# Order of SyncE's transfers where the two halves of the batch meet

## The reference

```
xn  = layernorm(x)
# attention-like part
xm  = xn * time_mix + shift_by_one_token(xn) * (1 - time_mix)
k   = exp(min(xm @ Wk.T, 60));  v = xm @ Wv.T;  r = xm @ Wr.T
wkv = decaying sum over earlier tokens of k*v      (per channel)
sk  = the same sum of k, + 1e-16
a   = (sigmoid(r) * wkv / sk) @ Wo.T
# FFN-like part
xf  = layernorm(xn) * ln_gamma + ln_beta
Wq  = Wf rounded to -1, 0, 1 by its mean absolute value beta
g   = max(abs(xf)) over ALL batches and tokens
f   = clip(xf * 128 / g, -128, 128) @ Wq * (g * beta / 128)
out = x + a + f
```

## Time and profile before

| | |
|---|---|
| runs shown | 918.77, 922.57, 922.42 us; median 922.42 |
| profiled execution | 919.68 us, of which the span from first to last instruction is 917.9 |
| PE busy | 880.4 us, 96% of the span |
| DVE, ACT, POOL busy | 761.5 (83%), 509.4 (56%), 188.1 us (20%) |
| mean granted TensorE clock | 0.992 |
| DMA | 107.13 MB, mean 117 GB/s |

### The profile page before, as it was taken

The page is one execution under the profiler, slowest core; times in us unless marked ns, Lnnn a source line. Parts: engine busy times, 40 slices in busy tenths (PEclk is TensorE's granted clock), DMA queues, the critical chain, the costliest instruction groups (busy, mean ns, idle before and its releaser), DMA issues.

```text
span 917.9 us, 12736 instructions
## 1 busy us (share of the span) xinstructions
PE 880.4 (96%) x3984; PEld 714.3 (78%) x3984; DVE 761.5 (83%) x1282; ACT 509.4 (56%) x830; POOL 188.1 (20%) x242
## 2 busy tenths in 40 slices
PE   2989999999999999999989999999999999999998
PEld 2768777787878777787867888888888888888886
DVE  5998988889798988889768887887878978789684
ACT  3674757657574757657445363554545544455441
POOL 5442333143242333140010020100201102011000
PEclk9999999999999999999999999999999999999999
DMA  8222415042422415043425443253332532334211
GB/s 275 105 81 80 150 41 186 15 149 69 149 80 77 152 46 181 14 151 112 154 97 185 138 144 111 80 192 137 110 115 107 194 137 92 104 137 138 92 47 46
DMA packets 59841, 107.13 MB, mean 117 GB/s; under 512 B 7712, under 2 KB 7712, under 8 KB 59808
## 3 DMA queue, kind: packets, MB, share of 16 engines
q1 hardware_dynamic: 59808, 106.73, 34.2%
HBM read 64.76 MB, written 41.96 MB: 116 GB/s over the span
## 4 chain that ended last, share of the span: by engine, by line
PE 63%; DVE 18%; issue 9%; ACT 4%; DMA 4%; POOL 1%; SPq 0%; DVEq 0%; ACTq 0%; POOLq 0%
PE kvr L483 12%; PE kvr L485 12%; PE kvr L484 12%; PE out_banks L519 6%; PE out_banks L521 6%; PE out_banks L498 5%; PE out_banks L501 5%; PE out_banks L500 5%; DVE scans L933 4%; DVE bn_stats L796 3%; PE transposed L441 2%; DMA other<-ffn_input 1%; DVE rwkv_lo L953 1%; DVE k_and_kv L923 1%; DVE k_and_kv L949 1%
## 5 line engine op out<-in xcount | busy, mean ns | idle before, releaser
L483 PE MATMUL kvr<-xm_hi,wk_hi 128*128 128x512 f32 x256 | 104.4, 408 | 7.2 <-DVE xm_lo L876 4.6
L1186 POOL TENSOR_TENSOR evacuated<-normed,mix_over_ffn_row 128x512 f32<-128x512 f32 x28 | 36.3, 1296 | 360.0 <-DVE ffn_lo L876 360.0
L483 PE MATMUL kvr<-xm_hi,wv_hi 128*128 128x512 f32 x256 | 102.9, 402 | 1.6 <-DVE k_and_kv L923 1.1
L483 PE MATMUL kvr<-xm_hi,wr_hi 128*128 128x512 f32 x256 | 103.3, 404 | 0.0
L498 PE MATMUL out_banks<-wo_hi,rwkv_hi 128*128 128x512 f32 x256 | 101.9, 398 | 0.5 <-DVE rwkv_lo L953 0.5
L485 PE MATMUL kvr<-xm_hi,wk_lo 128*128 128x512 f32 x256 | 101.5, 396 | 0.0
L501 PE MATMUL out_banks<-wo_hi,rwkv_lo 128*128 128x512 f32 x256 | 101.3, 396 | 0.0
L500 PE MATMUL out_banks<-wo_lo,rwkv_hi 128*128 128x512 f32 x256 | 101.2, 395 | 0.0
L519 PE MATMUL out_banks<-w_ternary,ffn_hi 128*128 128x512 f32 x256 | 100.0, 390 | 1.3 <-DVE ffn_lo L876 1.3
L484 PE MATMUL kvr<-xm_lo,wk_hi 128*128 128x512 f32 x256 | 100.9, 394 | 0.0
L485 PE MATMUL kvr<-xm_hi,wr_lo 128*128 128x512 f32 x256 | 100.4, 392 | 0.0
(11 more groups left out here) (125 smaller groups left out, 1910.7 us busy)
## 6 DMA issues: line engine op xcount, KB each, us to landing
other<-ffn_input SPq DMA_DIRECT2D x64, 256.0 KB, 5.4
x<-in_x SPq DMA_DIRECT2D x15, 1024.0 KB, 5.7
other<-in_x SPq DMA_DIRECT2D x8, 1024.0 KB, 5.7
ffn_input<-evacuated SPq DMA_DIRECT2D x32, 256.0 KB, 4.6
ffn_input<-parked SPq DMA_DIRECT2D x32, 256.0 KB, 2.1
attn_scratch<-x SPq DMA_DIRECT2D x8, 1024.0 KB, 4.3
parked<-attn_scratch SPq DMA_DIRECT2D x8, 1024.0 KB, 7.1
out<-parked SPq DMA_DIRECT2D x8, 1024.0 KB, 5.2
```

The lines of the kernel that those rows point to most:

```text
L483: nc.tensor.matmul(KVR[:, m, :], hi, XH[t][:, ch, :], start=(ch == 0), stop=False)
```

## The change

SP's program only; no other engine's changes, and no transfer is added, dropped or resized.

- The mix input of batch 4 (`load_mix_input(HALF, 1)` with its wait for the last transposes) moves from behind the load of x ahead of the wait for DVE's additions and the store of `x1`.
- The four loads of own0 for batch 4 move out of `batch_b` to right behind the store of `x1`.
- The load of `parked` (with its wait for the ternary matrix) stands between chunk 0 and chunk 1 of them.
- The load of the next x into `x1` comes last, behind chunk 3.

```diff
@@ last batch_a
                     for ch in range(CH):
                         sp.dma_start(ZA[:, ch, :], ffn_in[0, 0, ch]).then_inc(s_fld[ch], 16)
+                    sp.wait_ge(pe_t, slots_before(b, "A", len(SLOTS)))
+                    load_mix_input(HALF, 1)
                 sp.wait_ge(dve_out, BANKS + bank_use(b, "A", "attn1") + Q)
                 sp.dma_start(scratch_t[b, 1], X[1][:, :, :]).then_inc(s_xst[1], 16)
+                if is_last:
+                    for ch in range(CH):
+                        load_ffn_input(HALF, "own0", ch)
+                        if ch == 0:
+                            load_parked()
                 sp.wait_ge(s_xst[1], 16 * b + 16)
                 sp.dma_start(X[1][:, :, :], x_t[b + 1, 1]).then_inc(s_x[1], 16)
+
+            def load_parked():
+                sp.wait_ge(act_q, CH)
+                sp.dma_start(ZB[:, :, :], scratch_t[0, 0]).then_inc(s_park, 16)
@@ batch_b
-                for ch in range(CH):
-                    load_ffn_input(b, "own0", ch)
+                if b > HALF:
+                    for ch in range(CH):
+                        load_ffn_input(b, "own0", ch)
@@ behind the loop over half A
-            sp.wait_ge(pe_t, slots_before(HALF - 1, "A", len(SLOTS)))
-            load_mix_input(HALF, 1)
-            sp.wait_ge(act_q, CH)
-            sp.dma_start(ZB[:, :, :], scratch_t[0, 0]).then_inc(s_park, 16)
```

## The result

The changed kernel takes 912.93 us (median of 5 runs, 912.01 to 913.87), the kernel before 918.93 (5 runs, 917.11 to 922.57). The medians differ by 6.0 us. The ratio over all runs is 0.9921, 95% interval 0.9901 to 0.9941: faster by 0.8%, which would be 7.3 us of 918.93 (5.4 to 9.1). The profiled execution has a span of 911.1 us, where the one before had 917.9. Lines moved: L596, L599, L862, L876, L971 of before are L605, L608, L871, L885, L980.

What follows compares the result with a forecast made beforehand. TensorE was taken as the bound, full except where the halves meet, with ACT waiting 8.21 us for own0 chunk 0. Removing 6.66 us gave 913.0 from the profiled execution, 915.8 from the median; forecast 915.0, range 911.5 to 919.5.

Steps and rivals of the forecast that it cites:

- The sum: Total over all moved transfers at the meeting of the halves: 6.66 us less, 913.0 against the profiled execution.
- the window: Stretch from group 5 of batch 4 to its first output product: 35.68 us before, forecast 29.0 at clock 1.00.
- Batch 5 as the yardstick: Batch 5's same stretch, 29.02 us without TensorE gaps, gives the gain; shifted by 123.36 us, its engine starts show what is late next.
- The landing of chunk 0: Own0 chunk 0 behind the store of `x1`: lands 5.5 us after issue, about 451.5, bounds 449.9 and 458.8.
- The point of loss: ACT may start own0 chunk 0 as late as 458.35 without loss; 456.63 is 1.7 us early.
- The room for `parked`: At DVE's first addition of batch 4: `parked` costs from a landing at 464.1 + 1.7 = 465.8 on, us for us.
- The room for chunk 1: Own0 chunk 1 on ACT: even at 12.8 us landing, at most 2 of 6 us of room before group 5 ends.
- The share of the clock: TensorE before own0 chunk 3: of 3.2 us lost, 1.3 is a bracket behind DVE and 1.9 the lower clock.
- rival A: ACT and DVE late by themselves at the halves' meeting: only 2.5 to 3.5 us less, 919.4; chance 0.08.
- cost 0 on both ends: Mix input's move on SP: about 1.0 us of issue, covered by 15 us of SP idle time, so no cost.
- B: Own0 transfer hidden anyway or no faster, chunk 0 still landing at 464: 922.4, no change; chance 0.07.
- C: `parked` too late for DVE's addition: all 6.66 us gone at 472.4, 925 us total at 475; chance 0.05.

Runs made afterwards that it cites:

- 6: Changed kernel with `parked` ahead of own0 and all own0 chunks held until DVE's low part of slot 3: 915.32 against 919.9 us, ratio 0.9953.
- 7: Changed kernel with `parked` ahead of own0 and all own0 chunks held until TensorE ends group 5: 922.49 against 919.9 us, ratio 1.0031.
- 8: Changed kernel with the load of `parked` moved behind the next x: 912.68 against the kernel before's 919.9 us, ratio 0.9927.
- Experiment 1: Kernel before with only own0 chunk 0 of batch 4 moved right behind the store of `x1`: 914.04 against 920.49 us, ratio 0.9938.
- 9: Changed kernel with `parked` behind the next x and held until TensorE ends group 5: 918.16 against the kernel before's 919.95 us, ratio 0.9978.
- 10: Changed kernel with `parked` behind the next x and held until TensorE ends group 7: 922.47 against the kernel before's 919.95 us, ratio 1.0027.
- 4: Changed kernel with the mix input put back behind the next x: 914.58 against the kernel before's 920.49 us, ratio 0.9934.
- 5: As 4, plus one small POOL multiplication right behind the two reductions over partitions: 913.38 against the kernel before's 919.9 us, ratio 0.9932.

## Why the prediction was right

**The size and the place.** The sum said 6.66 us, all in the window. The window shows 6.66 and the span 6.8. Against the profiled execution the forecast was 913.0, and the profiled span came out at 911.1, as said. The median, 912.93, is 2.1 below the forecast of 915.0: I had leaned on two runs near 922.5, and with five the kernel before has its median at 918.93. The 6.66 lie between the 6.0 us of the medians and the 7.3 of the ratio.

**Batch 5 as the yardstick** held to the digit: 29.02 in both. Its shifted low part said 478.5, and after has 478.39. This was the strongest step, since it prices everything an engine does at once, by a stretch without the fault.

**The landing of chunk 0** was taken as 5.5 us from a store with a load behind the earlier trace rows and measured 5.4. The prediction cited from the Trainium skill ("DMA: Bandwidth & Descriptors", section "Queues, rings and completion order") that a completion waits for the earlier writes of its DMA engine. The runs agree: chunk 0 lands 0.2 us behind the store in after (451.37 and 451.15), takes 2.7 and 2.6 us with nothing ahead (6, 7), and `parked` behind it makes no more than 0.1 us of difference (8). They do not tell this rule from plain transfer time of the bytes ahead. The prediction took its lower bound of 4.3 from a store with nothing behind it; in after the store took 5.6.

**The point of loss** was reckoned as an ACT start of 458.35 and is 458.18 by the line above. The price, one for one, was right. The room for `parked` was reckoned as 1.7 us and is 2.3; DVE's timeline has 0.94 us of idle time of its own behind the addition in after, which may be what takes the rest; no run isolates it.

**The room for chunk 1** was put at 6 us, up to the end of group 5. Experiment 1 shows less: ACT took chunk 1 2.67 us after the start of group 5 and takes up that group's result at 2.92 in after, so the wait ended inside the room, and yet 1.08 us were lost, because DVE waits for other work of ACT behind chunk 1. In the change chunk 1 lands at 455.6, so nothing came of it.

**The share of the clock was wrong.** The prediction split the 6.66 us in stops and 1.9 us of lower clock. In experiment 6 the window has clock 1.00, in the kernel before 0.95, in 7 0.96, and all lie on one line; 9 and 10, at 1.00 and 0.91, have the same room, 2.28 and 2.30. So where the clock fell, the fall added nothing: TensorE ran slowly while the chain on ACT and DVE was late anyway, and the bracket ahead of chunk 3 was shorter for it. Had the clock stayed up before, by this line that bracket would have been an estimated 1.3 + 1.9 = 3.2 us and the total the same. It did no harm to the sum, which came from whole windows, but the prices of rival A, which had 1.9 us of clock on top, were too high.

**The mix input at "cost 0 on both ends"** was right for its cost and incomplete for its worth. In the change it gives POOL time for a 7.3 us delay that the prediction did not know, which was luck; put back, 1.07 us are lost (4), and returned once that delay is paid elsewhere (5). In the kernel before this delay was there too, hidden: POOL passed its waits at 459.93 and its first multiplication was not wanted before 472.4. So the prediction rightly added nothing for it, but without knowing why.

**The rivals.** A (ACT and DVE late by themselves) did not occur. B is refuted by the window of after, and by experiment 7: hold own0 back with the rest of the change in place, and the whole loss comes back and more. C is real as a mechanism, its room 0.6 us wider than reckoned; `parked` came at 455.0 (446.48 + 8.5). By the price list it costs from 466.1 on (463.86 + 2.28) and has eaten the whole gain at 472.8, 18 us later than it came; run 10 shows the far side.

No version came out faster than the changed kernel beyond the measurement. TensorE is full in it from 461.72 to 900, so an order of transfers has nothing left to give there.

## What to carry to other kernels

Where a loop's first round differs from the later ones, lay the same stretch of a later round beside it: the difference of the two windows is the gain to be had, and the shifted starts of the other engines say what would be late next. Order a queue by when each transfer is wanted, counting the bytes ahead of it and not its place in time; here 1.25 MB out of the way did nearly as much as the whole change. And price a late wait by its chain from the stop to the bound engine, with its room, rather than by adding up the gaps and the slow clock that it leaves behind.

## What was not expected of the hardware

- The first ordinary POOL instruction behind a reduction over partitions started 6.9 to 7.3 us after it could have been expected: 6.92 us behind the reductions (5), and 7.2 and 7.3 behind its configuration records, with its transfers landed (1, 4). The later multiplications of the same runs don't show it, and a small instruction placed earlier took it off the path. It shows as idle "issue", with no releaser.
- A granted clock of 0.95 over 35.68 us cost nothing here, because another chain was late anyway.
- POOL multiplications on top of DVE's recurrence stretched both sides in 4: the first two took 2.12 and 2.20 us against 1.3 (the third 1.28), and on DVE 2.25 and 2.40 against 1.19 and 1.28. They end by turns, at 475.35 (POOL), 476.43 (DVE), 477.51 (POOL), 478.76 (POOL) and 479.85 (DVE), each 1.1 to 1.25 us behind the one before. That looks like one at a time rather than both at half speed; no run isolates it.
- A 1 MB store takes 4.3 us from issue to landing alone, and 4.8 to 5.7 with loads issued right behind it, though it stands ahead of them.
